# Macaron stack: one-bank score tiles in the causal attention layers, and row maxima 26 instead of 32 tasks ahead in the full ones

## The reference, cut to what matters

```
full    att = q @ k^T / sqrt(4);  p = softmax(att);            o = p @ v   # [2,32,1024,1024], twice
causal  s = where(k <= q, q @ k^T / sqrt(8), -inf); p = softmax(s); o = p @ v   # [2,16,1024,1024], twice
```

## Time and profile before

| | |
|---|---|
| median of 3 runs | 3258.06 us (3256.76 to 3258.07) |
| the profiled execution: its time, its span | 3254.58 us, 3252.5 us |
| PE busy | 2875.6 us (88%) |
| DVE busy | 2296.2 us (71%) |
| ACT busy | 1871.8 us (58%) |
| POOL busy | 511.2 us (16%) |
| DMA | 121.69 MB, mean 37 GB/s |

### The profile page before, as it was taken

The page is one execution under the profiler, slowest core; times in us unless marked ns, Lnnn a source line. Parts: engine busy times, 40 slices in busy tenths (PEclk is TensorE's granted clock), DMA queues, the critical chain, the costliest instruction groups (busy, mean ns, idle before and its releaser), DMA issues. The chain is left out here.

```text
span 3252.5 us, 43802 instructions
## 1 busy us (share of the span) xinstructions
PE 2875.6 (88%) x15996; PEld 1089.9 (34%) x16044; DVE 2296.2 (71%) x3000; ACT 1871.8 (58%) x3785; POOL 511.2 (16%) x832
## 2 busy tenths in 40 slices
PE   5999989899999997888968999999987899777788
PEld 2443434222222223533321222222255333253345
DVE  5454555899999994566649999999926766554951
ACT  2214322488888886456654888888846466554012
POOL 0000000200000100222221000110003222232630
PEclk9999999699999999899987999999999799988979
DMA  3210031300000000211012000000001211100000
GB/s 113 94 50 1 20 98 56 123 20 20 19 19 19 19 12 28 78 56 39 33 47 104 19 19 19 19 19 19 25 15 33 85 43 44 32 1 24 0 0 14
DMA packets 67506, 121.69 MB, mean 37 GB/s; under 512 B 16083, under 2 KB 42708, under 8 KB 64125
## 3 DMA queue, kind: packets, MB, share of 16 engines
q1 hardware_dynamic: 67292, 118.90, 11.3%
HBM read 95.38 MB, written 23.48 MB: 37 GB/s over the span
## 5 line engine op out<-in xcount | busy, mean ns | idle before, releaser
L1279 DVE TENSOR_REDUCE arena<-ps 128x1 f32<-128x1024 f32 (+7 forms) x1536 | 1573.1, 1064 | 239.6 <-PE ps L904 158.8
L1157 ACT ACTIVATE arena<-ps 128x512 f32<-128x512 f32 (+3 forms) x2816 | 1382.6, 573 | 406.9 <-PE ps L967 345.9
L898 PE MATMUL ps<-arena 61*128 61x512 bf16 (+4 forms) x2816 | 953.7, 384 | 67.0 <-DVE arena L1279 35.7
L967 PE MATMUL ps<-arena 64*128 64x512 bf16 (+4 forms) x2768 | 735.1, 371 | 66.4 <-ACT arena L1157 39.1
L924 PE MATMUL ps<-arena 128*32 128x512 f32 (+3 forms) x5632 | 712.9, 578 | 0.7 <-POOL arena L1238 0.3
L967 PEld LDWEIGHTS ps<-arena 64*128 64x128 bf16 (+1 forms) x2816 | 206.2, 95 | 769.1 <-ACT arena L1157 543.3
L898 PEld LDWEIGHTS ps<-arena 61*128 61x128 bf16 (+1 forms) x2816 | 259.3, 96 | 412.0 <-DVE arena L1279 356.6
L337 PE MATMUL ps<-xnT,moe_up 128*128 128x512 f32 x480 | 231.8, 608 | 0.0
L453 ACT ACTIVATE arena<-ps 128x512 f32<-128x512 f32 x120 | 71.4, 597 | 224.4 <-PE ps L337 224.4
L523 DVE TENSOR_TENSOR arena<-arena,ps 128x512 f32<-128x512 f32 x120 | 82.2, 687 | 158.2 <-ACT arena L453 129.7
L1207 POOL TENSOR_TENSOR arena<-arena,ones 16x128 bf16<-16x128 f32 x96 | 42.8, 446 | 845.1 <-ACT arena L1142 781.8
(11 more groups left out here) (228 smaller groups left out, 2703.4 us busy)
## 6 DMA issues: line engine op xcount, KB each, us to landing
arena<-m_w SPq DMA_DIRECT2D x32, 512.0 KB, 3.5
arena<-f_q SPq DMA_DIRECT2D x60, 144.0 KB
arena<-f_k SPq DMA_DIRECT2D x180, 48.0 KB
arena<-m_w SPq DMA_DIRECT2D x64, 128.0 KB, 3.9
arena<-in_w SPq DMA_DIRECT2D x4, 2048.0 KB
arena<-a_q SPq DMA_DIRECT2D x14, 576.0 KB
arena<-a_k SPq DMA_DIRECT2D x42, 192.0 KB
a_q<-arena SPq DMA_DIRECT2D x44, 96.0 KB, 2.0
```

The costliest lines, as they stand in the source:

```text
L898: last = nc.tensor.matmul(at[:, k0 // CHUNK, 0:n], score_rows(Qop[par], j, slice(q0, q0 + P)), score_rows(Kop[par], j, slice(k0, k0 + n)), ...
L967: nc.tensor.matmul(ps[:, ring_bank(item), off:CHUNK], shifted_rows(Kop[par], j, slice(kb * P, (kb + 1) * P)), shifted_rows(Qop[par], j, sl ...
L1157: nc.scalar.activation(pr[:, (at % 2) * 4 + j, off:CHUNK], ps[:, ring_bank(item), off:CHUNK], ACT.Exp).then_inc(s.ex, 1)
L1279: nc.vector.tensor_reduce(mq[:, half, j * 4 + qb:j * 4 + qb + 1], src, AXX, ALU.max).then_inc(s.sread, 1)
```

## The change

It does two things.

**Causal layers, first half.** A tile of at most 512 columns now takes one bank instead of a pair, and the four banks 0 to 3 go round: `score_bank` gives bank k % 4 for tasks 0 to 15. `reuse` says how many tasks back the bank's last user is: 4 within the first half (2, 3, 3 for its first three tasks, whose banks were last used by wide tiles of the unit before), and 3 then 2 at the passage to the second half. So PE may be up to four tasks ahead of DVE there, not two. Second half and full layers keep the two pairs.

**Full layers.** `EARLY` is 26 instead of 32: the prologue runs 26 tasks, each unit's steps run tasks 26 to 57 counted from the unit's own first, and the last unit runs the 6 that remain in its steps 0 to 2. As maxima of a half are complete later, `TURN_AT` is (4, 1) for both halves: steps 4 and 12. On SP the load for unit u+2 goes ahead of `put_max` of half 1. PE's wait for the next unit's operands moves to the task that first reads them, in step 3.

```diff
-            TURN_AT = ((2, 1), (2, 1)) if full else ((0, 3), (1, 1))
+            TURN_AT = ((4, 1), (4, 1)) if full else ((0, 3), (1, 1))
+            EARLY = 26 if full else 32
 ...
                 def unit(u, third, par, ahead2, ahead1):
+                    if ahead2 and full:
+                        sp.wait_ge(s.st, u * 4 * NS + 1)
+                        load(u + 2, (par + 2) % 3)
                     put_max(u, par, 1)
-                    if ahead2:
+                    if ahead2 and not full:
                         sp.wait_ge(s.st, u * 4 * NS + 1)
                         load(u + 2, (par + 2) % 3)
 ...
+            def score_bank(half, k):
+                if not full and half == 0:
+                    return S_SLOT + k % 4
+                return S_SLOT + 2 * (k % 2)
+
+            def reuse(half, k):
+                if full or half and k != 0:
+                    return 2
+                if half:
+                    return 3
+                return (2, 3, 3, 4)[min(k, 3)]
 ...
-                    if n_task >= 2 and piece in (None, 0):
-                        pe.wait_ge(s.sread, n_task - 1)
+                    if n_task >= reuse(half, k) and piece in (None, 0):
+                        pe.wait_ge(s.sread, n_task - reuse(half, k) + 1)
-                    b = S_SLOT + 2 * (k % 2)
+                    b = score_bank(half, k)
 ...
-                        if at == 0 and ahead1:
-                            pe.wait_ge(operands[(par + 1) % 3], placed(u + 1))
+                        per = 16 // len(halves[qc])
+                        for k in range(per * kb, per * kb + per):
+                            n_task = 32 * u + EARLY + 16 * qc + k
+                            if n_task >= 32 * UNITS:
+                                continue
+                            if n_task == 32 * (u + 1):
+                                pe.wait_ge(operands[(par + 1) % 3], placed(u + 1))
+                            todo += [(n_task, 0), (n_task, 1)] if SIDES == 2 else [(n_task, None)]
 ...
-                for k in range(16):
-                    scores(-1, 0, 1, k)
+                for k in range(16, EARLY):
+                    scores(k)
```

More of the change, by code:

```diff
@@ L882, in project_values, with scores @@
                     last.then_inc(s.vps, 1)
-                def scores(u, par, half, k, piece=None):
+                def scores(n_task, piece=None):
+                    par, half, k = n_task // 32 % 3, n_task % 32 // 16, n_task % 16
                     j, qb = s_tasks(half)[k]
-                    n_task = (u + 1) * 32 + 16 * half + k
-                    if n_task >= 2 and piece in (None, 0):
-                        pe.wait_ge(s.sread, n_task - 1)
+                    if n_task >= reuse(half, k) and piece in (None, 0):
+                        pe.wait_ge(s.sread, n_task - reuse(half, k) + 1)
                     q0 = half * CHUNK + qb * P
                     width = SEQ if full else q0 + P
-                    b = S_SLOT + 2 * (k % 2)
+                    b = score_bank(half, k)
                     at = ps[:, b:b + 2, :]
@@ L949, in unit @@
                             pe.wait_ge(max_placed[qc], 16 * SIDES * (u + 1) + 1)
-                        if at == 0 and ahead1:
-                            pe.wait_ge(operands[(par + 1) % 3], placed(u + 1))
                         todo = []
[L953 to L959, removed]
+                        per = 16 // len(halves[qc])
[6 more added lines that the diff above has]
+                            todo += [(n_task, 0), (n_task, 1)] if SIDES == 2 else [(n_task, None)]
                         def run(task):
-                            half, k, piece = task
-                            scores(u, (par + 1) % 3, half, k, piece=piece)
+                            n_task, piece = task
+                            scores(n_task, piece=piece)
                         for i, j in enumerate(ST_ORDER):
@@ L1014, in tensor @@
                 for k in range(16):
-                    scores(-1, 0, 0, k)
+                    scores(k)
                 if not full:
```

## The result

| | before | after |
|---|---|---|
| median of 4 runs, us | 3258.07 (3256.76 to 3259.6) | 3221.27 (3216.9 to 3225.47) |
| ratio | | 0.9887 (95% interval 0.987 to 0.9904) |
| profiled execution, span | 3254.58, 3252.5 | 3219.71, 3217.8 |

36.8 us less by the medians, 34.9 by the profiled executions, where 44.4 were forecast. The time, 3221.3, lies in the whole range (3203 to 3233), 7 us from the predicted 3214 and at the very end of the forecast's own 3207 to 3221.

The account below looks back on a forecast made before the run. PE's depth-two handshake with DVE was taken to bound causal steps 0 to 3, DVE's maxima the full prologue. Gains of 35.8 + 8.6 = 44.4 us from 3258.06 gave 3213.7, said as 3214; range 3203 to 3233, the forecast's own 3207 to 3221.

Parts of the forecast that it names:

- Causal waits gone, and no new one in their place: Causal steps 0 to 3: PE's waits for DVE go, nothing else becomes late; 2.56 us a unit, 35.8 us in all.
- rival 1: Causal steps 1 to 4: the wait moves to maxima rows, DVE or ACT; half of 35.8 left, 3231.6 us; chance 0.14.
- Nothing for the causal prologue: Causal prologue: four banks counted as no gain, since ACT's start hangs on stores; if wrong, 2.6 us a layer.
- Full prologue 7.06 us: Full layers' prologue: loses 6 tasks of 1.176 us, 7.06 us, with the start not held by the maxima.
- The last unit, 2.75 us: Full layers' last unit: six more maxima delay DVE's quotient, and PE at out_project, by 7.2 - 4.45 = 2.75 us.
- full part: Full layers: prologue gain less last unit's delay, 4.3 us a layer, 8.6 us in both; bounds 0 to 14.1.
- Turns later and load ahead, at nothing: Full layers' steady units: turns 4.8 us later and load before the maxima's write cause no stall; 1.8 to 2.8 us spare.
- Rival 3: Full layers: maxima's write stands behind the load and step 8 stalls; slower, 48 us middle case, 174 us worst; chance 0.05.
- Rival 2: Full layers bring nothing, their start held or the last unit's delay felt in full; 3222.3 us; chance 0.12.
- causal term: Causal layers, steps 0 to 3: 14 units at 2.56 us, 35.8 us gained; bounds nothing to 39 us.

Follow-up runs that it names:

- e5: Causal one-bank tiles in four banks, but PE's depth kept at 2, full layers as before the change; 3258.15 us, ratio 0.9995 to the kernel before.
- e9: Causal part alone with PE at most three tasks ahead of DVE instead of four, full layers as before; 3226.01 us, ratio 0.9911 to the kernel before.
- e2: New kernel with the causal layers back at two pairs and depth two, so the full layers' part alone; 3252.9 us, ratio 0.9987 to the kernel before.
- e3: New kernel with the 16 outer_apply operations issued one by one between the maxima; 3212.69 us, 8.6 below the new kernel.
- e6: New kernel with the full layers' turns two steps later, at steps 6 and 14; 3352.19 us in one run, against 3223.12 of the new kernel.
- e7: New kernel with SP's load put back behind put_max in the full layers; 3224.12 us, ratio 0.9891 to the kernel before.
- e4: New kernel with 16 filler matmuls of 512 columns on PE ahead of the last unit's first out_project; 3221.01 us, ratio 0.9889 to the kernel before.
- e11: New kernel with outer_apply spread between the maxima, plus EARLY 25 instead of 26, turns unmoved; 3309.28 us, ratio 1.0158 to the kernel before.
- e1: New kernel with the full layers as before, so the causal one-bank tiles alone; 3224.0 us, ratio 0.9899 to the kernel before.
- e10: Kernel before the change with only the outer_apply operations spread between the maxima; 3256.77 us, ratio 1.0002 to the kernel before.
- e8: New kernel with outer_apply spread, plus EARLY 24 and the turn two score tiles later in its step; 3225.92 us, ratio 0.991 to the kernel before.
- after_again: The new kernel run once more, unchanged, beside two follow-up kernels; 3223.12 us, ratio 0.9892 to the kernel before.

## Why the prediction was right and where it was off

- **Causal waits gone, and no new one in their place: right.** The waits for DVE fell from 19.6 to 2.2 us in a layer, rival 1's holds didn't come but for the 0.22 us at 1591.95, and e5 and e9 show that the depth is the cause. Its term was mis-sized by a tenth: 2.30 instead of 2.56 us a unit, as steps 1 to 3 each keep a changeover of about 0.08 us that a sum of tile intervals leaves out (0.92 against 0.84 in step 3). Over 14 units that is 3.6 us.
- **Nothing for the causal prologue: right.** ACT's first exponent there still waits for the stores (21.6 us in the waits view of after).
- **Full prologue 7.06 us: right** (7.30, 6.97).
- **The last unit, 2.75 us: the step that failed.** Its mechanism was right, DVE in order with the quotient behind six more maxima, but it measured 6.0 and 6.3 us. Two things were missing. First, the delay was 3.7, not 2.75. Counted from the copy, DVE came to the quotient 2.40 us behind it before and 10.55 after: 8.15 us later, not the 7.2 of six tasks, and 8.15 - 4.45 is 3.7. Of the 0.95 us more, 0.74 are `outer_apply`, whose last three operations ran long while POOL cut the maxima of the turn that the change had moved there. That POOL is the cause is read from the times in the traces of the new kernel and e2; no run has it apart. Second, PE's 4.5 us of idle had a price of its own: the clock fell to 1.2 GHz for some 7 us, 2.3 us more in this execution and about 6 in others. So the full part is 1.9 us instead of 8.6 from these two intervals and the prologues. e3, whose last units are 8.4 us shorter together, brings it to some 10.
- **Turns later and load ahead, at nothing: right**, with 2.3 us to spare; e6 shows what it costs when they are gone (129 us), e7 that the order isn't needed. Rival 3 didn't come; the 10.4 us that priced it belong to a write of a causal layer (at 1582.7), and in the steady units of the full layers no write of the kernel before took over 1.9. The write behind the load took 1.9 instead of 1.4 us to the return's issue, inside the cover. What the Trainium skill says (DMA: Bandwidth & Descriptors, section Queues, rings and completion order), that a completion stands behind the earlier writes of its DMA engine, agrees in sign; the size, 0.5 us, is the trace's.
- **Rival 2** came out nearer in number than the forecast (3222.3 and 3214 against 3221.3) and half in mechanism: the last unit's delay took most of the full part. So the forecast had the waits right, and its time is right only within the range. The causal term 3.5 us too large and the full one 6.2 too large are the 9.7 us by which the spans missed the forecast.

What the last unit costs is best seen as one table, made of PE's wait before the first `out_project` and the length of that half unit (f1 and f2 of each trace; e4, with its filler, apart; e11's halves hold some of its longer steps, about 0.4 us):

```
PE's wait, us   half unit, us    kernel
0.73 to 0.89    23.17 to 23.34   before (both), e1 f1, e5 f2, e9 f2
0.85, 0.85      23.73, 27.62     e11 f1, e11 f2
0.99, 1.05      23.43, 23.49     e10 f2, e9 f1
1.11            24.85            e1 f2
1.34, 1.34      25.32, 25.06     e3
1.42, 1.45      25.40, 29.20     e5 f1, e10 f1
2.01, 2.01      26.70, 25.90     e8
4.25            29.45, 29.53     e6
4.50            29.2 to 29.5     after (both), e2 (both), after_again f1, e7 f2
4.50            33.0             after_again f2, e7 f1
0.93 + filler   28.18, 28.52     e4
```

Open: why equal waits give 23.7 or 27.6, 25.4 or 29.2, and 29.3 or 33.0 us. In each such pair the longer one is at half clock for longer, and the price follows that time: 2.3 us beyond the delay for 6.1 us at half clock behind the wait (after, f1), 3.9 for 10.2 (e11 f2), 6.0 for 15.9 (e7 f1), some 0.4 us for each. What decides how long it is wasn't tried.

## What to carry to other kernels

When two engines hand tiles to each other and neither is full, look for a wait that names the reader of the tile two back: one or two tiles more of depth remove it, and the layout of the banks is only what makes room. A prologue made shorter by doing less ahead comes back in the last unit; there, follow each engine's order behind the work that remains, and move what needs no input (here `outer_apply`) ahead of it, which gave the best version, 3212.7 us. When a lead is changed, check that it keeps the phase between the two streams that share the array, that the first rows of maxima land before the shorter prologue ends (in e8 they didn't), and the place of the turn within its step.

## What the runs showed of the hardware that was not expected

- The granted clock fell to 0.5 behind waits of PE between 0.85 and 4.5 us in an otherwise busy stretch, and stayed at 1.00 behind 0.80 us (before, f1), 0.85 us (e11, f1) and 1.05 us (e9, f1). The smallest wait followed by a fall was e11's 0.85 us in f2. Over all kernels the fall cost 1.3 to 6 us beyond the delay itself, up to 4.6 times the wait (3.9 us in e11's f2). No rule is drawn from it, since equal waits were followed by unequal stretches at the low level.
- 3.6 us of filler matmuls, followed by 0.93 us of idle, moved the fall from 1238 to 1242, left it half as long, and didn't prevent it.
- Two bf16 score matmuls on the two halves of the array's rows start at the same instant (729.96 both) and cost together what one costs; with the order shifted by one the step grows from 2.39 to 2.60 us, and ACT's idle from 0.33 to 0.54.
- Three operations of DVE on 128x128 f32 took 0.57 to 0.60 us instead of 0.34 while POOL was cutting maxima (after, 1233.06 to 1234.66, and the same in e2); in the kernel before, with POOL idle, all 16 took 0.34. No run isolates it.
- A small write issued 3 us behind a load of eight DMAs took 1.9 us to its return's issue instead of 1.4. In the causal layer a1, with larger loads, the write of the maxima took 3.5 us in the median and 14.1 at most, and in the steady units PE waited for the return by no more than 0.2 us.
